# A decoder layer on one core: the q and k projections two steps ahead of their scores, ScalarE and VectorE taking the turned output first in a step, GpSimd making the low half of the next tokens

## What is computed

```python
x = layernorm(x + attn(x))            # 16 heads of 16, causal
x = layernorm(x + xattn(x, ctx))      # cross-attention on 120 context rows, softmax over them
x = layernorm(x + ffn(x))             # channel mix with the token before

# attn: q, k, v = x@Wq.T+bq, x@Wk.T+bk, x@Wv.T+bv, split into heads
q_lr = einsum('bhtd,hdr->bhtr', q, Wq_lsr)      # rank 32
k_lr = einsum('bhtd,hdr->bhtr', k, Wk_lsr)
scores = einsum('bhir,bhjr->bhij', q_lr, k_lr) * 32**-0.5
y = softmax(causal(scores)) @ v ;  return heads_together(y) @ Wo.T + bo

# ffn: xr, xk = mixes of x and the token before; r = sigmoid(xr @ Wr.T)
return r * ((relu(xk @ Wk.T) ** 2) @ Wv.T)
```

## Time and profile before

| | us |
|---|---|
| three runs | 1104.71, 1097.24, 1111.92 |
| median | 1104.71 |
| the profiled execution | 1103.24 |
| its span, first to last instruction | 1101.5 |
| its mean granted TensorE clock | 0.954 |

### The profile page before, as it was taken

How to read it: one execution, slowest core, us unless ns; L and a number is a source line. 1 busy time by engine, 2 the same in 40 slices (tenths; PEclk the granted TensorE clock), 3 DMA queues, 4 the chain that set the end, 5 groups by cost and what they waited for, 6 DMA issues and landing times.

```text
span 1101.5 us, 24092 instructions
## 1 busy us (share of the span) xinstructions
PE 980.6 (89%) x8740; PEld 761.0 (69%) x8804; DVE 809.7 (74%) x1725; ACT 582.0 (53%) x1121; POOL 285.3 (26%) x537
## 2 busy tenths in 40 slices
PE   4667899999999999999999999999999999998863
PEld 4446677777777777777776777777777777776652
DVE  5335788788788787878787878878888787876453
ACT  1123455556665555566565555666555555565532
POOL 5000122222233222223322222223322223222332
PEclk9678999999999998999999999999999999999886
DMA  7664565666565566664655566655655666660000
GB/s 178 117 109 102 110 112 105 126 131 125 114 121 102 112 111 103 131 126 107 119 112 109 108 106 131 131 116 119 111 114 120 108 103 128 131 122 25 21 11 19
DMA packets 114784, 118.57 MB, mean 108 GB/s; under 512 B 20649, under 2 KB 98283, under 8 KB 114667
## 3 DMA queue, kind: packets, MB, share of 16 engines
q1 hardware_dynamic: 114667, 117.03, 54.4%
HBM read 74.00 MB, written 41.94 MB: 105 GB/s over the span
## 4 chain that ended last, share of the span: by engine, by line
DMA 38%; PE 26%; SPq 16%; ACT 8%; issue 7%; POOL 2%; DVE 2%; ACTq 0%; POOLq 0%; DVEq 0%
DMA parts_dram<-parts 25%; SPq L358 12%; DMA stack<-parts_dram 12%; PE ps_m L482 5%; PE ps_m L474 3%; PE ps_t L500 3%; PE ps_s L500 3%; ACT sum L703 2%; PE ps_t L506 2%; ACT x L679 2%; PE ps_o L552 2%; ACT yT_hi L696 1%; SPq L329 1%; PE ps_s L506 1%; ACT parts L671 1%
## 5 line engine op out<-in xcount | busy, mean ns | idle before, releaser
L662 ACT ACTIVATE p<-ps_t 128x1024 f32<-128x1024 f32 x192 | 196.6, 1024 | 129.3 <-PE ps_t L506 110.5
L856 DVE TENSOR_REDUCE row_max<-ps_s 128x4 f32<-128x1024 f32 (+1 forms) x192 | 232.8, 1213 | 43.2 <-PE ps_s L506 28.5
L1054 POOL TENSOR_TENSOR var<-mv,eps 128x2 f32<-128x2 f32 x96 | 18.8, 196 | 602.0 <-DVE mv L879 602.0
L500 PE MATMUL ps_s<-stack 48*128 48x128 f32 (+1 forms) x1024 | 109.3, 313 | 46.4 <-DMA stack<-parts_dram 41.3
L500 PEld LDWEIGHTS ps_s<-stack 48*128 48x128 f32 x1024 | 73.7, 191 | 82.4 <-DMA stack<-parts_dram 46.4
L500 PEld LDWEIGHTS ps_t<-stack 50*128 50x128 f32 x1024 | 73.7, 191 | 61.9 <-issue 43.3
L500 PE MATMUL ps_t<-stack 50*128 50x128 f32 (+1 forms) x1024 | 109.5, 314 | 5.3 <-ACT p L662 3.2
L772 ACT COPY kxT<-ps_m 128x240 f32<-128x240 f32 x32 | 11.5, 358 | 189.7 <-PE ps_m L454 189.7
L552 PE MATMUL ps_o<-p,v_pad 128*32 128x256 f32 (+1 forms) x2048 | 96.3, 329 | 0.0
L552 PEld LDWEIGHTS ps_o<-p,v_pad 128*32 128x32 f32 x2048 | 57.5, 109 | 39.3 <-issue 17.4
L1080 POOL TENSOR_TENSOR xr_lo<-dx,xr_hi 128x512 fp32r<-128x512 f32 x32 | 40.8, 1274 | 141.9 <-ACT xr_hi L736 141.9
(11 more groups left out here) (167 smaller groups left out, 2801.8 us busy)
## 6 DMA issues: line engine op xcount, KB each, us to landing
stack<-parts_dram SPq DMA_DIRECT2D x384, 128.0 KB, 4.4
parts_dram<-parts SPq DMA_DIRECT2D x64, 512.0 KB, 5.3
x_in<-in_x_turned SPq DMA_DIRECT2D x32, 256.0 KB, 2.9
x_res<-in_x SPq DMA_DIRECT2D x32, 256.0 KB, 3.2
out_x<-sum SPq DMA_DIRECT2D x64, 128.0 KB, 1.8
ctxT<-in_ctx_turned SPq DMA_DIRECT2D x32, 120.0 KB, 5.6
stack<-shift_parts SPq DMA_DIRECT2D x128, 8.0 KB
p<-in_Wq SPq DMA_DIRECT2D x1, 256.0 KB, 2.8
```

The source lines that it names most:

```text
L500: nc.tensor.matmul(o, left[b.slot][r0:r0 + rows_n, h // 2, rows_at:rows_at + P], right[b.slot][r0:r0 + rows_n, h // 2, col:col + width], s ...
L662: nc.scalar.activation(p[c][:], ps_t[:], ACT.Exp).then_inc(exp_done[c], 1)
L856: nc.vector.tensor_reduce(row_max[:, tile, :, j0:j0 + nj], ps_s[:].rearrange("p (g j w) -> p g j w", j=nj, g=2), AX_X, ALU.max) \
```

## The change

The skews become 0, 2, 3, 4, 5: q and k are projected two steps ahead of their scores, and there are 37 steps instead of 36. Six edits go with it.

1. SP's step is put in a new order: save q, output of the step before's FFN, save k, x_in of the next step, x_res, ctxT, the shift rows, and last the twelve stack loads, six of q and six of k. A save waits, from the fourth batch on, for the loads of three batches before.
2. xT_hi of the next batch is made by ScalarE between g_sb and kxT (`x_hi(at + 1)`), that of batch 0 ahead of everything.
3. xT_lo of the next batch is made by GpSimd at the end of its step (`x_lo(at + 1)`), and no longer by VectorE.
4. ScalarE's step begins with yT_hi, ahead of exp(0).
5. VectorE's step begins with yT_lo, ahead of row_maxima(0).
6. GpSimd makes the ones of slot 0 among its constants and those of slots 1 and 2 after x_lo(0); SP waits for each slot's ones ahead of loading k's stack, and no longer for consts_ready. GpSimd waits for setup_taken between steps 0 and 1.

```diff
-IN, SCORES, PROBS, CROSS, FFN = range(5)
+IN, SCORES, PROBS, CROSS, FFN = 0, 2, 3, 4, 5
...
+            def save_parts(b, s, ready):
+                if b.n >= RING:
+                    sp.wait_ge(stack_loaded[b.slot], Batch(b.n - RING, IN).dma_count(12))
+                sp.wait_ge(v_[ready], b.n + 1)
+                sp.dma_start(parts_dram[s][b.slot]...., parts[s][:].bitcast(F32)).then_inc(parts_saved[s][b.slot], 16)
+            def load_stack(b, s, which):
+                sp.wait_ge(parts_saved[s][b.slot], b.dma_count(1))
...
             def step(at):
+                if live(at, IN):
+                    save_parts(b, 0, "q_lo")
+                if live(at - 1, FFN):
+                    c = Batch(at - 1, FFN)
+                    for j in range(NT):
+                        sp.wait_ge(x3_ready[j], c.n + 1)
+                        sp.dma_start(tokens(out, c.n)[j * P:(j + 1) * P, :], x3[:, j, :]).then_inc(out_saved, 16)
+                if live(at, IN):
+                    save_parts(b, 1, "k_lo")
+                if live(at + 1, IN):
+                    sp.wait_ge(g_["xT_lo"], b.n + 1)
+                    sp.dma_start(x_in[:], tokens(x_turned, b.n + 1)....).then_inc(x_loaded, 16)
...
+                if live(at, IN):
+                    if b.n >= RING:
+                        before_it = Batch(b.n - RING, IN)
+                        sp.wait_ge(t_filled, before_it.chunks_done(T_ORDER, T_ORDER[-1]))
+                    load_stack(b, 0, (0, 0, 1))
+                    if b.n < RING:
+                        sp.wait_ge(ones_ready[b.n], 2)
+                    load_stack(b, 1, (0, 1, 0))
```

ScalarE and VectorE:

```diff
+            def x_hi(n):
+                if not live(n, IN):
+                    return
+                b = Batch(n, IN)
+                act.wait_ge(x_loaded, (b.n + 1) * 16)
+                wait(act, filled["f_v"], b.n - 2)
+                nc.scalar.copy(flat(xT[b.slot][0]), flat(x_in)).then_inc(a_["xT_hi"], 1)
...
-                if on[IN]:
-                    act.wait_ge(x_loaded, (A.n + 1) * 16)
-                    wait(act, filled["f_v"], A.n - 2)
-                    nc.scalar.copy(flat(xT[A.slot][0]), flat(x_in)).then_inc(a_["xT_hi"], 1)
+                if on[CROSS]:
+                    act.wait_ge(y_turned[0], X.n + 1)
+                    act.wait_ge(y_turned[1], X.n + 1)
+                    wait(act, filled["f_z1"], X.n)
+                    nc.scalar.copy(flat(yT[0]), flat(y32T)).then_inc(a_["yT_hi"], 1)
                 exp(0)
...
+                x_hi(at + 1)
                 if on[PROBS]:
                     act.wait_ge(filled["f_kx"], Pb.n + 1)
...
-                if on[IN]:
-                    dve.wait_ge(a_["xT_hi"], A.n + 1)
-                    wait(dve, filled["f_v"], A.n - 2)
-                    nc.vector.tensor_tensor(flat(xT[A.slot][1]), flat(x_in), flat(xT[A.slot][0]).bitcast(F32),
-                                            ALU.subtract).then_inc(v_["xT_lo"], 1)
-                row_maxima(0)
-                if live(at - 1, FFN):
-                    stats(2, Batch(at - 1, FFN), sum3, v_["sum3_done"])
                 if on[CROSS]:
                     dve.wait_ge(a_["yT_hi"], X.n + 1)
                     wait(dve, filled["f_z1"], X.n)
                     nc.vector.tensor_tensor(flat(yT[1]), flat(y32T), flat(yT[0]).bitcast(F32), ALU.subtract) \
                         .then_inc(v_["yT_lo"], 1)
+                row_maxima(0)
+                if live(at - 1, FFN):
+                    stats(2, Batch(at - 1, FFN), sum3, v_["sum3_done"])
                 row_maxima(2)
```

GpSimd:

```diff
+            def x_lo(n):
+                if not live(n, IN):
+                    return
+                b = Batch(n, IN)
+                pool.wait_ge(a_["xT_hi"], b.n + 1)
+                wait(pool, filled["f_v"], b.n - 2)
+                g.tensor_tensor(xT[b.slot][1][:], x_in[:], xT[b.slot][0][:].bitcast(F32), ALU.subtract) \
+                    .then_inc(g_["xT_lo"], 1)
...
                 if on[CROSS]:
                     inverse_deviation(1, X)
+                x_lo(at + 1)
...
+            x_lo(0)
+            pool.wait_ge(g_["xT_lo"], 1)
+            for r in range(1, RING):
+                ones_rows(r)
+            run_steps(step, ahead=1, between=other_weights)
```

More of the change, by code:

```diff
@@ L218, in decoder_layer @@
         consts_ready = sem("consts_ready")
+        ones_ready = [sem(f"ones_ready{r}") for r in range(RING)]
         consts_step = sem("consts_step")
@@ L325, in tokens @@
                 return ap[n, :, :]
-            def load_x(b):
-                wait(sp, v_["xT_lo"], b.n)
-                sp.dma_start(x_in[:], tokens(x_turned, b.n).rearrange("(k p) t -> p k t", p=P)).then_inc(x_loaded, 16)
+            def save_parts(b, s, ready):
+                if b.n >= RING:
+                    sp.wait_ge(stack_loaded[b.slot], Batch(b.n - RING, IN).dma_count(12))
+                sp.wait_ge(v_[ready], b.n + 1)
+                sp.dma_start(parts_dram[s][b.slot].rearrange("(a p) w t -> p a w t", p=P), parts[s][:].bitcast(F32)) \
+                    .then_inc(parts_saved[s][b.slot], 16)
+            def load_stack(b, s, which):
+                sp.wait_ge(parts_saved[s][b.slot], b.dma_count(1))
+                for g in range(2):
+                    for row, part in enumerate(which):
+                        src = parts_dram[s][b.slot].rearrange("(j g d) w t -> g w d j t", g=2, d=DH)[g, part]
+                        r0 = 64 * g + DH * row
+                        sp.dma_start(stack[s][b.slot][r0:r0 + DH].bitcast(F32), src) \
+                            .then_inc(stack_loaded[b.slot], 16)
             def step(at):
-                if live(at, IN) and at > 0:
-                    load_x(Batch(at, IN))
-                at = at - 1
                 b = Batch(at, IN)
+                if live(at, IN):
[9 more added lines that the diff above has]
+                    sp.wait_ge(g_["xT_lo"], b.n + 1)
+                    sp.dma_start(x_in[:], tokens(x_turned, b.n + 1).rearrange("(k p) t -> p k t", p=P)).then_inc(x_loaded, 16)
                 if live(at, PROBS):
@@ L340, in step @@
                     sp.dma_start(x_res[:], tokens(x, c.n).rearrange("(j p) c -> p j c", p=P)).then_inc(x_res_loaded, 16)
[L341 to L359, removed]
                 if live(at, SCORES):
@@ L515, in step @@
             def step(at):
-                A, Sb, Pb, X, F = (Batch(at, s) for s in range(5))
-                on = [live(at, s) for s in range(5)]
+                A, Sb, Pb, X, F = (Batch(at, s) for s in (IN, SCORES, PROBS, CROSS, FFN))
+                on = {s: live(at, s) for s in (IN, SCORES, PROBS, CROSS, FFN)}
                 def S(c):
@@ L691, in step @@
                     normalise(1, X1, x2, sum2, "x2_ready")
-                if on[CROSS]:
-                    act.wait_ge(y_turned[0], X.n + 1)
-                    act.wait_ge(y_turned[1], X.n + 1)
-                    wait(act, filled["f_z1"], X.n)
-                    nc.scalar.copy(flat(yT[0]), flat(y32T)).then_inc(a_["yT_hi"], 1)
                 if on[IN]:
```

35 lines of the change are left out of this document (16 added, 19 removed).

## The result

The changed kernel takes 1043.16 us, the median of 4 runs from 1039.44 to 1044.40; the kernel before, on the same chip, 1106.16 (4 runs). The profiled execution took 1044.40, so it stands 58.8 under the profiled one of before (1103.24). The sum said 46.0.

A forecast was written before the change was run, and what follows sets the result against it. TensorE bounds the kernel, with a DMA chain lasting just longer than what lies between k and the next scores. Terms sum to -46.0 from 1103.24, giving 1057.2; with 1.5 to the median, 1058.7 us; range 1046 to 1086.

The forecast's parts named there:

- the two without q and k: Late steps with 24 matmuls less but S(2) waiting for row_max(0): 29.2 each, -2.0 and -1.7.
- front, to kx of batch 0: Program start: the extra step costs +1.3, Tr(0) of batch 0 at 67.8 instead of 66.45; bounds -5 to +12.
- 29.45 + 0.33 issue, taken as 29.8: Each of 26 full steps: TensorE busy time plus issue; 774.8 against 806.9 together, -32.1.
- the 2.3 us that the prediction gave to the clock: In the 26 full steps before the change, TensorE was busy some 2.3 us longer through its clock.
- The stack wait: Ahead of a step's first scores: TensorE's wait for stack<-parts_dram, 18.4 us in 26 steps, goes wholly.
- bounds 0 to 0.9 a step: Shift rows now ahead of the stack loads on SP: cost to Tr(0) of 0 to 0.9 a step, taken as 0.
- The turned output first: Step start, yT_hi and yT_lo earlier: the Wo product's wait of 0.37 a step goes; S(2) in time by 0.35.
- x's low half: xT_lo on GpSimd at K+3.62 (K: start of kx group), in time for q by 0.44; cost taken as 0.
- Rival A: GpSimd keeps the shared port, x_res's add ahead of yT_lo: S(2) waits 0.85 in 27 steps, 1082; chance 0.20.
- Rival C: Port lost again and the clock falls in many steps: slower, up to 1149; chance 0.06.
- D: SP's queue runs so late that loads are again awaited, nothing won: 1103; chance 0.04.
- rival B: Front: extra step not hidden, x(2) waits for batch 1's stack traffic, q(2) some 20 us later: 1079; chance 0.08.

The follow-up runs named there:

- experiment 1: Changed kernel with the yT instructions of ScalarE and VectorE back in their old, later places: 1070.24 us, 0.9691 of the kernel before.
- experiment 5: Changed kernel keeping only the new skews, SP's order and the ones' set-up, x's halves and turned output as before: 1066.44 us, 0.967 of the kernel before.
- experiment 9: The repeat: the changed kernel once more with no edit: 1043.11 us, 0.9449 of the kernel before.
- experiment 6: Changed kernel with the old skews and SP's old order, all other edits kept: 1090.56 us, 0.99 of the kernel before.
- experiment 4: Changed kernel with SP loading the stacks ahead of the shift rows: 1230.04 us, 1.1131 of the kernel before.
- experiment 2: Changed kernel with only VectorE's order undone, row_maxima(0) and the statistics ahead of yT_lo: 1039.57 us, 0.941 of the kernel before.
- experiment 10: Changed kernel with SP loading the next x_in first in its step, ahead of both saves: 1040.12 us, 0.9408 of the kernel before.
- experiment 8: Changed kernel with row_maxima(0) ahead of yT_lo only in the steps without q and k: 1041.80 us, 0.9427 of the kernel before.
- experiment 11: Changed kernel with x_in loaded first by SP and VectorE's old order, row_maxima(0) ahead of yT_lo: 1033.99 us, 0.9362 of the kernel before.
- experiment 3: Changed kernel with GpSimd's two operations swapped, x_res's add ahead of xT_lo: 1086.12 us, 0.9828 of the kernel before.
- experiment 7: Changed kernel with xT_lo on VectorE again, behind yT_lo and ahead of row_maxima(0): 1070.66 us, 0.9707 of the kernel before.

## Why the prediction came out as it did

The mechanism was right and so was the sign; the size of one term was off, and it alone puts the time below the range. By the terms of the sum, in us of the profiled executions:

| term | forecast | measured |
|---|---|---|
| 26 full steps | -32.1 | 806.9 to 761.4: -45.5 |
| two steps before them | -9.1 | 33.4 to 26.4, 32.4 to 29.3: -10.1 |
| the two without q and k | -3.7 | 31.2 and 30.9 to 28.7 each: -4.7 |
| 28.9 (no scores), and the last two | -2.4 | 28.9 to 25.3, the rest 51.5 to 51.1: -4.0 |
| front, to kx of batch 0 | +1.3 | 86.3 to 91.8: +5.5 |
| sum | -46.0 | -58.8 |

Of the 12.8 us between the sums the full steps make 13.4 and the three terms at the ends 3.6. The front, 4.2 the other way, hid part of that, by luck.

**The step that failed** is "29.45 + 0.33 issue, taken as 29.8". A full step takes 29.28, so 0.5 a step, 13.4 us in all, more than was forecast. The floor was read from the busy column of the 30.00 step, and that column held waits. Here are five starts of that step of the kernel before (kx at 243.81), then the same five of a step of the changed one (kx at 440.31):

```profile
247.48 0.60 PE L506 MATMUL ps_t<-mask_t,identb 128*128 128x512 bf16 x2
248.12 0.36 PE L474 MATMUL ps_m<-xT_hi,hi_Wq 128*128 128x256 f32 x1
...
249.73 0.50 PE L500 MATMUL ps_s<-stack 48*128 48x256 f32 x4
...
250.92 0.39 PE L511 MATMUL ps_t<-mask_t,identb 128*128 128x256 bf16 x2
251.50 0.36 PE L482 MATMUL ps_m<-hi_Wo,yT_hi 128*128 128x256 f32 x1 [0.19 <-DVE yT_lo L927]
```

```profile
443.98 0.61 PE L510 MATMUL ps_t<-mask_t,identb 128*128 128x512 bf16 x2
444.24 0.47 PE L478 MATMUL ps_m<-xT_hi,hi_Wq 128*128 128x256 f32 x1
...
445.96 0.50 PE L504 MATMUL ps_s<-stack 48*128 48x256 f32 x4
...
447.14 0.39 PE L515 MATMUL ps_t<-mask_t,identb 128*128 128x256 bf16 x2
447.29 0.37 PE L486 MATMUL ps_m<-hi_Wo,yT_hi 128*128 128x256 f32 x1
```

From the mask of Tr(0) to S(2) it is 2.25 before and 1.98 after: 0.27 was a wait of q, for xT_lo, with nothing in the idle column. From the mask of Tr(2) to Wo it is 0.58 and 0.15: 0.43 was a wait, of which the column shows 0.19. Every other group of the two steps stands at the same distance from the one ahead of it (to 0.02 where the first product of a group has its record). Together 0.70, and 30.00 less 0.70 is the 29.3 measured. The modelled end of a mask's matmul (0.39 and 0.60 after its start) reached over the wait. Experiments 1 and 5 bring 0.70 back by the one wait (1) or by both (5), and the step is 29.98 in each. So with the turned output late it is the end of yT_lo that sets the step, and a wait of q only takes its part out of that of the Wo product. The 0.33 of "issue" was no part of the error: it is TensorE at work without records (experiment 9), so it belonged into the floor. For the same reason the 2.3 us that the prediction gave to the clock are too few: 768.1 busy and 8.5 without records are 15.2 more than the 761.4 of after, and that is hidden waits and lower clock together.

**The stack wait.** Right: gone wholly, and experiments 5 and 6 show that the skews with SP's order are what removes it; no run has the one without the other. The shift rows' place was right with 0 taken, but "bounds 0 to 0.9 a step" was too narrow: on the other side of the stack loads they cost 6.6 (experiment 4). The bound was read from an order in which q's and k's loads go out in two blocks, each when its parts are ready; with all twelve just ahead, a price from that row did not hold.

**The turned output first.** Right in kind; worth 0.70 and not 0.37, as above. It is ScalarE's place that brings it (experiment 2). VectorE's place isn't needed for it: with row_maxima(0) ahead of it yT_lo is still early enough.

**x's low half.** q and S(2) do not wait. The margins were forecast as 0.44 and 0.35; in the step start above they are 0.29 (xT_lo ends at K+3.64, q starts at K+3.93) and 0.27 (row_max(0) ends at K+5.37, S(2) starts at K+5.64). The swap (1.47 a step) and VectorE (0.94) show how near the margin is.

**Rival A.** Falls for this kernel: yT_lo keeps 0.69 in all its steps. VectorE goes between GpSimd's two operations, and the one behind it pays, 1.79 for x_res's add with yT_lo beside it and 1.28 without (experiment 2), where nobody waits for it. By the Trainium skill (SBUF — State Buffer, "Who interferes with whom"), whoever issues first holds the shared pair for the whole instruction; the trace agrees, since the add's record is 0.51 longer, most of yT_lo's 0.69. The 0.1 that yT_lo was to lose to x's subtraction by the same rule does not show: its record starts 0.10 before that of xT_lo ends, and is as long as alone. But the rival's price is real. The margin is 0.06 us at the step start shown, and where the add was 0.11 ahead instead (experiment 10), the step took 1.14 more, where 0.85 was put down for it. **Rival C** falls with it: clock 1.00 in all full steps. **D** falls: SP's order is not late.

**B, the front.** Not as rival B had it: q(2) began at 45.05, where 45 was forecast, and Tr(0) of batch 0 at 67.98 by its stack matmuls, where 67.8 was. But +1.3 to kx of batch 0 became +5.5. From Tr(0) to kx the kernel before took 19.90 at a clock of 0.94:

```profile
66.45:86.35 19.90, 17.97 (x181) 12.67 (x181) 11.11 (x16) 8.47 (x12) 1.24 (x1) 0.94 0.45 101
```

The changed kernel took 23.81 there at 0.72 in this profile and 21.28 at 0.86 in the repeat, for the same work (180 matmuls). The other profiles with its order fall on the same two values: 21.2 to 21.3 at 0.85 or 0.86 (experiments 2, 5, 8, 11), 23.8 to 23.9 at 0.72 (1, 3, 7, 10). So of the 4.2 that were not forecast 3.9 stand behind Tr(0). 2.5 of them go with the clock, which differs from one execution of the same kernel to the next; for the other 1.4 the clock is lower too, but no run separates it. What makes the clock rise sooner or later stays open.

**Steps without q and k.** Right: 2.16 idle each, where 2.0 was forecast. The clock did better than allowed for in the steps behind them (0.93 against 0.82).

## What to carry over

Take the floor of a step from start to start, between groups that nothing makes wait, and compare the starts around each suspected wait: a column of idle time that is made from modelled ends hides waits of some tenths, here 0.5 of 30 us. Before an "issue" gap is believed, compare the counts of matmuls and weight loads. And of two blocks of transfers in one queue, the small ones that someone waits for go ahead of the large ones that are read a step later.

## What the runs showed of the hardware that was not expected

- Four small loads issued behind twelve stack loads on one queue: 7.1 us from the end of their issue to the matmul that waited for them, against at most 3.9 with the twelve behind them. That order made the kernel 11% slower than the one before and 18% slower than the changed one (1230.0 over 1043.2).
- yT_lo on VectorE arrives while GpSimd is in an operation and goes in ahead of GpSimd's next one, in either order of GpSimd's two, and that next one lasts 1.76 to 1.81 in the full steps instead of 1.28. Its record starts 0.03 to 0.06 us ahead of that next one. In the two steps where it started 0.11 behind (experiments 8 and 10), GpSimd's kept 1.27 and yT_lo took 1.71 instead of 0.69.
- From the first Tr(0) to kx of batch 0, with the same work of TensorE, the mean granted clock was 0.72 or 0.85 to 0.86 and the stretch 23.8 to 23.9 or 21.2 to 21.3 us, in two executions of the same kernel one of each.
